# The causal mask of a decayed attention on GpSimd instead of TensorE, and new order weights for both attentions

## The reference

```python
att = softmax(where(causal, q @ k.T / 4, -inf))        # first attention
y   = (att * decay_weight_matrix(T)) @ v               # 1 - (lag/496)**(1/e) behind 15 ones, 0 from lag 511
x   = x + y @ W_proj
x   = x + ffn(layernorm(x))                            # binarized weights, GELU, 1024 hidden
x   = x + layernorm(causal_attention(layernorm(x)) @ Wo + bo) * gamma + beta
x   = x + ffn(layernorm(x))
```

## Time and profile before

| | us |
|---|---|
| median of 3 runs | 2536.53 (2535.64 to 2544.38) |
| the profiled execution | 2545.83 |
| its span, first to last instruction | 2544.1 |
| PE, DVE, ACT, POOL busy | 2319.2, 1961.9, 1469.6, 1020.4 |
| first attention, 150 to 1092 | 942 |
| second attention, 1405 to 2294 | 889 |

### The profile page before, as it was taken

One profiled execution on the slowest core, in us unless ns is written; L12 is line 12 of the kernel. 1 busy time (PEld: TensorE's weight loads), 2 busy tenths in 40 slices (PEclk: granted clock), 3 DMA queues, 4 the chain that ended last, 5 costly groups with the idle time before them and its releaser, 6 DMA issues. The chain is left out here.

```text
span 2544.1 us, 49747 instructions
## 1 busy us (share of the span) xinstructions
PE 2319.2 (91%) x16288; PEld 1345.7 (53%) x16288; DVE 1961.9 (77%) x4826; ACT 1469.6 (58%) x3293; POOL 1020.4 (40%) x1269
## 2 busy tenths in 40 slices
PE   4979999999999989969997799999999998994887
PEld 2545555555555545547765455455454554443666
DVE  5668888888888869756663799898898895914886
ACT  1228687785867777523332357777777776671333
POOL 0038789887878867922211101010010010014452
PEclk8979999999999989989998789999999999996999
DMA  4662122130302140043324611230221314003210
GB/s 153 245 174 68 36 61 64 36 89 11 85 19 77 53 96 11 10 131 119 118 97 134 137 37 42 54 90 23 77 68 32 86 50 104 6 13 120 67 42 33
DMA packets 161902, 188.67 MB, mean 74 GB/s; under 512 B 69360, under 2 KB 92656, under 8 KB 160880
## 3 DMA queue, kind: packets, MB, share of 16 engines
q1 hardware_dynamic: 160304, 180.25, 25.1%
q10 hardware_dynamic: 1344, 5.24, 0.6%
HBM read 114.37 MB, written 69.99 MB: 72 GB/s over the span
## 5 line engine op out<-in xcount | busy, mean ns | idle before, releaser
L886 POOL TENSOR_TENSOR att_a_wd<-att_a_wt,decay 128x256 f32<-128x256 f32 (+3 forms) x896 | 748.4, 872 | 183.4 <-ACT att_a_wt L913 90.9
L913 ACT ACTIVATE att_b_wt<-att_b_ps 128x512 f32<-128x512 f32 (+3 forms) x1280 | 586.7, 542 | 263.9 <-PE att_b_ps L1045 261.5
L953 DVE TENSOR_REDUCE att_a_mpart<-att_a_pm 128x1 f32<-128x512 f32 x768 | 497.5, 683 | 72.7 <-PE att_a_pm L1025 71.4
L953 DVE TENSOR_REDUCE att_b_mpart<-att_b_pm 128x1 f32<-128x512 f32 x768 | 493.8, 683 | 56.9 <-PE att_b_pm L1025 55.5
L913 ACT ACTIVATE att_a_wt<-att_a_ps 128x512 f32<-128x512 f32 (+3 forms) x896 | 415.6, 516 | 182.6 <-PE att_a_ps L1045 178.8
L896 POOL TENSOR_SCALAR_AFFINE_SELECT att_b_wt<-att_b_wt 128x512 f32<-128x512 f32 x128 | 81.3, 635 | 797.5 <-ACT att_b_wt L913 797.5
L1045 PE MATMUL att_b_ps<-att_b_mx,ones_row 64*128 64x512 f32 (+3 forms) x1280 | 364.9, 370 | 0.0
L1025 PE MATMUL att_a_pm<-att_a_kop,att_a_qop 64*128 64x512 f32 (+3 forms) x1024 | 313.5, 423 | 23.7 <-DMA att_a_qop<-qk 12.6
L1038 PE MATMUL att_b_ps<-att_b_qop,att_b_kop 64*128 64x512 f32 (+3 forms) x1024 | 331.9, 434 | 1.4 <-ACT att_b_wt L913 0.7
L1025 PE MATMUL att_b_pm<-att_b_kop,att_b_qop 64*128 64x512 f32 (+3 forms) x1024 | 291.5, 391 | 14.5 <-DMA att_b_qop<-qk 11.4
L1073 PE MATMUL att_b_po<-att_b_wt,att_b_va 128*17 128x512 f32 (+3 forms) x2560 | 292.9, 535 | 0.9 <-POOL att_b_wt L896 0.7
(11 more groups left out here) (183 smaller groups left out, 3540.4 us busy)
## 6 DMA issues: line engine op xcount, KB each, us to landing
att_a_kop<-qk SPq DMA_DIRECT2D x224, 64.0 KB, 2.9
att_b_kop<-qk SPq DMA_DIRECT2D x224, 64.0 KB, 2.9
att_a_qop<-qk SPq DMA_DIRECT2D x216, 64.0 KB, 3.0
att_b_qop<-qk SPq DMA_DIRECT2D x216, 64.0 KB, 2.9
qk<-qkv_a_qk_hi SPq DMA_DIRECT2D x8, 1024.0 KB, 4.0
qk<-qkv_a_qk_lo SPq DMA_DIRECT2D x8, 1024.0 KB, 6.4
y<-att_a_y SPq DMA_DIRECT2D x32, 256.0 KB, 2.3
y_ahead<-y SPq DMA_DIRECT2D x32, 256.0 KB
```

The source lines that it names most:

```text
L886: pool.tensor_tensor(wd[:, v % WD, h, a:z], wt[:, v % buffers, h, a:z], keep["decay"][:, u:u + z - a], ALU.mult).then_inc(w_decayed, 1)
L913: act.activation(wt[:, v % buffers, h, a:CH], pe_[:, n % EBANKS, 0:CH - a], ACT.Exp)\
L953: dve.tensor_reduce(mpart[:, g % 2, c, piece, u:u + 1], pm[:, n % MBANKS, 0:w], AX.X, ALU.max, negate=True).then_inc(m_reduced, 1)
```

## The change

In the decayed attention the mask matmuls go, with the tiles `tri` and `identr`. ScalarE exponentiates the unmasked scores, and GpSimd sets the part above the diagonal of a diagonal block to 0, for four heads at once, as it already does in the other attention. It therefore waits for all four exponentials of such a block, selects, waits for its own select, and then multiplies the four heads by the decay. Blocks off the diagonal are multiplied head by head as before. PO waits for the select on diagonal blocks. The class `Plan` gets the new steps of GpSimd and loses the mask matmuls, and its weights are others.

```diff
-MAXIMUM, FAR, EXP = 75.0, 690.0, (60.0, 0.84)
-TUNED = {True: (100.0, 2, 0.51, (800.0, 200.0, 200.0, 300.0), 0.1, False),
-         False: (30.0, 4, 0.56, (500.0, 200.0, 200.0, 300.0), 0.2, False)}
+MAXIMUM, FAR, EXP = 100.0, 790.0, (170.0, 0.714)
+TUNED = {True: (200.0, 7, 0.49, (400.0, 200.0, 200.0, 0.0), 0.0, False),
+         False: (0.0, 2, 0.51, (300.0, 0.0, 200.0, -600.0), 0.0, True)}
...
         @block.gpsimd
             for item in PLAN:
-                if item[0] == "X" and decayed:
-                    _, g, n, c, kb, h = item
-                    v = n // GH
-                    a, z, u = band_columns(c, kb)
-                    pool.wait_ge(e_weights, n + 1 + EBANKS)
-
-                    pool.wait_ge(pv_done, max(0, v + 1 - WD) + buffers)
-                    pool.tensor_tensor(wd[:, v % WD, h, a:z], wt[:, v % buffers, h, a:z],
-                                       keep["decay"][:, u:u + z - a], ALU.mult).then_inc(w_decayed, 1)
...
+                if item[0] != "X":
+                    continue
+                _, g, n, c, kb, h = item
+                v, diagonal = n // GH, kb >= TB * c
+                if diagonal and n % GH < GH - 1 or not decayed and not diagonal:
+                    continue
+
+                pool.wait_ge(e_weights, n + 1 + EBANKS)
+                if diagonal:
                     pool.sem_inc(w_turn, 1)
-                    block = wt[:, n // GH % buffers, :, P * (kb - TB * c):P * (kb - TB * c + 1)]
+                    block = wt[:, v % buffers, :, P * (kb - TB * c):P * (kb - TB * c + 1)]
                     pool.affine_select(out=block, in_=block, compare_op=ALU.is_ge, fill=0.0, base=0,
                                        pattern=[[0, GH], [1, P]], channel_multiplier=-1).then_inc(w_masked, 1)
+                if decayed:
+                    a, z, u = band_columns(c, kb)
+                    if diagonal:
+                        pool.wait_ge(w_masked, MASKED[v])
+                    pool.wait_ge(pv_done, max(0, v + 1 - WD) + buffers)
+                    for j in range(GH) if diagonal else (h,):
+                        pool.tensor_tensor(wd[:, v % WD, j, a:z], wt[:, v % buffers, j, a:z],
+                                           keep["decay"][:, u:u + z - a], ALU.mult).then_inc(w_decayed, 1)
...
                 if kind == "X":
-                    for i in range(2 if decayed and kb >= TB * c else 0):
-                        tri = keep["tri"][rows, (0, 1, 2, 0)[2 * (h // (GH // 2)) + i], :]
-                        pe.matmul(pe_[:, n % EBANKS, HALF * i:HALF * (i + 1)], tri, keep["identr"][rows, rows],
-                                  start=False, stop=False)
                     mm = pe.matmul(pe_[:, n % EBANKS, 0:CH - a], keep["ones_row"][rows, :], mx[rows, par, c, j, a:CH],
                                    start=False, stop=True)
...
                     pe.wait_ge(e_weights, GH * (v + 1) + EBANKS)
                     if first:
                         pe.wait_ge(o_kept, done(g, c))
+                    if kb >= TB * c:
+                        pe.wait_ge(w_masked, MASKED[v])
```

More of the change, by code:

```diff
@@ L137, in _ @@
             pool.memset(ident[:, :], 0.0).then_inc(zeroed, 1)
-            pool.memset(identr[:, :].bitcast(F32), 0.0).then_inc(zeroed, 1)
-            pool.memset(keep["tri"][:, :, :].bitcast(F32), 0.0).then_inc(zeroed, 1)
             pool.memset(keep["ones_row"][:, :].bitcast(F32), 1.0).then_inc(zeroed, 1)
@@ L142, in _ @@
             pool.memset(keep["ones_strip"][:, HD:STRIP], 1.0).then_inc(zeroed, 1)
-            pool.wait_ge(zeroed, 7)
-            for m in (ident, identr):
+            pool.wait_ge(zeroed, 5)
+            for m in (ident,):
                 pool.affine_select(out=m[:, :], in_=m[:, :].bitcast(F32), compare_op=ALU.not_equal, fill=1.0, base=0,
@@ L149, in _ @@
                                fill=MASK, base=0, pattern=[[-1, P]], channel_multiplier=1).then_inc(ident_ready, 1)
-            for n, base in enumerate((0, HALF, -HALF)):
-                pool.affine_select(out=keep["tri"][:, n, :], in_=keep["tri"][:, n, :].bitcast(F32),
-                                   compare_op=ALU.is_ge, fill=MASK, base=base, pattern=[[-1, P]],
-                                   channel_multiplier=1).then_inc(ident_ready, 1)
         @block.vector
@@ L588, in subtract @@
         a = P * max(0, kb - TB * c)
-        diagonal = self.decayed and kb >= TB * c
-        end = self.run(HEADS[k] // (GH // 2), start, CH - a + 2 * diagonal * (HALF + 48))
+        end = self.run(HEADS[k] // (GH // 2), start, CH - a)
         ready = max(end, self.done.get(v - self.buffers, 0.0))
@@ L596, in subtract @@
         self.weights[v] = self.act + 100.0
-        if self.decayed:
-            a, z, _ = band_columns(c, kb)
-            self.pool = max(self.pool, self.weights[v], self.done.get(v - self.wd, 0.0)) + 160.0 + 2.1 * (z - a)
-            self.decays[v] = self.pool + 120.0
-        elif kb >= TB * c and k == GH - 1:
+        if kb >= TB * c and k == GH - 1:
             self.pool = max(self.pool, self.weights[v]) + 650.0
             self.weights[v] = self.pool + 120.0
+        if self.decayed and (kb < TB * c or k == GH - 1):
+            a, z, _ = band_columns(c, kb)
+            count = GH if kb >= TB * c else 1
+            self.pool = max(self.pool, self.weights[v], self.done.get(v - self.wd, 0.0)) + count * (160.0 + 2.1 * (z - a))
+            self.decays[v] = self.pool + 120.0
     def product(self, start, kind, v, columns):
```

10 lines of the change are left out of this document (2 added, 8 removed).

## The result

| | us |
|---|---|
| before, median of 11 runs | 2539.16 (2527.28 to 2545.18) |
| after, median of 11 runs | 2552.22 (2550.38 to 2570.41) |
| ratio | 1.0075, 95% interval 1.0051 to 1.0099 |
| after, measured once more beside 20 runs of before | 1.0033, interval 1.0012 to 1.0054 |

The change made the kernel slower, by 0.3 to 0.75%. The forecast was 1.0% faster. The time lies in the predicted range, the sign does not.

What follows compares the result with a forecast made beforehand. The prediction took VectorE to set the pace of both attentions. From the profiled 2545.83 us, -10 (first attention) and -16 (second) gave 2519.8; less 9.3 for the median, the forecast was 2510.5 us, range 2470 to 2565.

Steps and rivals of the forecast that it cites:

- What bounds the kernel: Both attentions: they run at VectorE's pace, with some 11 to 12% lost to uneven feeding by TensorE.
- Second attention, -16 us: Second attention: TensorE's new order saves a quarter of VectorE's 62 us of waiting, 16 us; a loss bounded by +10.
- the 40 us: Second attention: a move of more than 40 us either way would show its reading mis-sized.
- First attention, -10 us: First attention: 112 us of new GpSimd work and waits, less 122 us of closed idle time, gives -10 us.
- The select's 81.3 us: First attention: 128 selects on GpSimd at 0.635 us each add 81.3 us.
- Its self-wait: First attention: GpSimd waits 0.24 us for its own result after each of 128 selects, 31 us, bounds 0 to 61.
- I take four fifths: First attention: of 152 us of GpSimd idle time that can close, four fifths close, 122 us.
- TensorE's relief: First attention: dropping 1024 mask matmuls is worth nothing to 56 us at the stage's end; no term of its own.
- Doubling of the loss: First attention: fuller GpSimd doubles what VectorE's two-input operations lose, +24 us in the even stretch, hidden under GpSimd.
- Setup, 0: Setup: six fewer GpSimd instructions for mask and identity change nothing; without cover under 2 us.
- the third rival: First attention: GpSimd multiplying without a break starves VectorE's two-input operations, +50 us there, 2576 us in all; chance 0.22.
- the order brings nothing: Both attentions: the two effects cancel or the second attention's order gains nothing, 2525 to 2547 us; chance 0.20.

Runs made afterwards that it cites:

- 15: b_order_old with VectorE's plain maxima of the second attention reading 256 of 512 columns; second attention 877.8 us.
- 17: b_order_old with two matmuls of zeros ahead of each subtraction of a diagonal block of the second attention; 2588.54 us, second attention 944.6.
- number 7: b_order_old with two matmuls of zeros ahead of each subtraction of a diagonal block of the first attention; 2576.82 us beside 2537.82 of before.
- after_again: The changed kernel unaltered, measured again against before; ratio 1.0033 (1.0012 to 1.0054), second attention 906.8 us.
- b_weigh_back: The changed kernel with the second attention's weigh put back from 0.0 to 0.2; ratio 1.0114 (1.0091 to 1.0136), second attention 931.6 us.
- number 6: The kernel before, mask matmuls kept, with the new weights and prices in the first attention only; ratio 1.0208, first attention 989.8 us.
- number 8: b_order_old with the first attention's select cut to 8 columns of one head; 2528.82 us beside 2537.82 of before, first attention 919.0.
- b_order_old: The changed kernel with the second attention's weights and prices of before; ratio 0.9938 (0.9916 to 0.9959), measured again 0.9947 (0.9920 to 0.9975).
- b_order_new_only: The kernel before with the new weights and prices in the second attention alone; ratio 1.0076 (1.0055 to 1.0098), second attention 903.8 us.

## Why the prediction was wrong

**What bounds the kernel.** The step that failed is the first one: "today both attentions run at VectorE's pace". It was read from the releasers of VectorE's idle time. But that VectorE waits for TensorE says that TensorE is late. The warning that a full row of pipelined matmuls is no proof was taken for an argument against TensorE; it is none for or against. Runs 15 and 17 show otherwise for the second attention: a quarter of VectorE's work can go from its middle without one matmul more getting done, and 1024 matmuls of zeros cost 57 us. For the first attention number 7 shows that TensorE's work counts there too; whether VectorE's does was not tested.

**Second attention, -16 us; measured +21.6.** Sign and size wrong, and the bound of +10 for a loss too. The term "I take a quarter, 16 us" of VectorE's 62 us of waiting rests on that step: it took a new order of TensorE as a gain for VectorE and put what the order does to TensorE's own waits at nothing. The move of 21.6 us lies under the 40 us that the prediction had set as its sign of being wrong; that sign was too wide. If TensorE sets the pace, an order can only gain by keeping TensorE from waiting. Here are its loads' waits in 500 us of the middle, of before:

```profile
PEld att_b_ps L1038 <- ACT att_b_wt L913: 156.9, 301, 0.9
PEld att_b_po L1073 <- ACT att_b_wt L913: 30.1, 87, 0.4
PEld att_b_po L1073 <- issue: 25.8, 84, 0.4
PEld att_b_ps L1038 <- issue: 6.0, 13, 0.9
PEld att_b_pm L1025 <- DVE att_b_mpart L957: 3.9, 6, 0.9
```

and of after:

```profile
PEld att_b_ps L1033 <- ACT att_b_wt L908: 148.9, 324, 0.9
PEld att_b_po L1066 <- issue: 31.1, 95, 0.4
PEld att_b_po L1066 <- ACT att_b_wt L908: 29.4, 87, 0.4
PEld att_b_pm L1020 <- DVE att_b_mpart L948: 10.0, 19, 0.9
PEld att_b_pm L1020 <- DVE att_b_mpart L952: 9.6, 15, 0.9
```

Together they are 222.7 us before and, with two small rows, 233.2 after. That is 10.5 more: 15.7 more for maxima that wait for their bank, 5.2 less for all the rest. Over the whole stage it is 411 against 439 us, with 24 and 63 for the maxima, and after_again has 438. TensorE does 3813 matmuls for 3920, which is 500 x (1 - 3813 / 3920) = 13.6 us less work. So the waits are of the size of the loss, and the new place is the maxima's bank. That is a match, not a proof: with VectorE's maxima halved those waits are still 13.8 us plus 6.8 of "issue", so they are not there because VectorE is slow, and b_weigh_back is the slowest order with a sum of only 227.8. By groups of heads, told by the ends of their value products, the five groups in the middle take 104.6 us each against 102.0 on average, 13 us in all, and the last two 129 + 97 against 112 + 107, another 7. **Open** is which property of the new list makes the maxima late. Two weights (the preference for closing first, the prices) were not undone alone.

**First attention, -10 us; measured -16.6**, and -10 between the median of 14 profiles (926) and the mean of the two with the old code (938.4 and 933.8), of which the spread of 17 us leaves the size open. Term by term:
- The select's 81.3 us: 81.6. Its self-wait: 128 x 0.08 = 10 us, not 31.
- The records of selects and multiplications overlap a little, so that GpSimd's busy time rose by 75 us (755.61 to 831.06). With the self-wait 86 us were added, not 112.
- "I take four fifths" of 152 us closable idle, 122 us: of 183.4 us of idle time 91.2 are left, and 10 of these are the self-wait. So 102 closed, two thirds of 152, and 86 - 102 = -16, as the stage has it. Both terms came out smaller, by 26 and 20 us, and their difference came out near the forecast because they did so together.
- TensorE's relief was "worth between nothing and 56 us" and no term of the sum. Under the new order it is worth about 43 (number 7), and the new weights with the mask matmuls kept lose 51 (number 6). It belonged in the sum. GpSimd's fullness, on which the sum was built, limits little (number 8).

**VectorE and GpSimd in each other's way.** Doubling of the loss was wrong in sign: lines 964, 972 and 997 average 567, 407 and 494 ns in the even stretch of after, where the earlier trace rows had 675, 460 and 1403. VectorE's busy time in the stage was to go "a little up" and fell by 46 us (800.18 to 754.21) at the same 1979 instructions: these three lines took 73.5 us before and 30.5 after, and one operation alone took 32.66 of the 73.5. What this is worth in time no run prices. Nor did the 32.66 us last "the whole time in which GpSimd multiplied without a break": the operation ended at 1087.39, and GpSimd went on to 1089.00.

```profile
L964 DVE TENSOR_TENSOR att_a_ffactor<-att_a_mneg,att_a_mpart 128x16 f32<-128x16 f32 x18 | 9.7, 567 | 0.4
L997 DVE TENSOR_TENSOR att_a_scol<-att_a_scol,att_a_frow 128x32 f32<-128x32 f32 x11 | 5.4, 494 | 0.0
L972 DVE TENSOR_TENSOR att_a_ffactor<-att_a_ffactor,att_a_fsum 128x32 f32<-128x32 f32 (+1 forms) x12 | 4.9, 407 | 0.0
```

**Setup, 0:** the first attention starts 1.1 us later in this pair and at 150.8 to 152.9 us over all runs, so nothing can be told from it. TensorE's total fell by 14.1 us (2319.2 to 2305.1), under the 133 as said.

**The rivals.** The kernel became slower, but not by the third rival: GpSimd starved nobody. The second, "the order brings nothing", was nearest with its 2525 to 2547 us, and it too allowed for no loss by the order. The missing rival was that the new order can make TensorE wait more.

That the time fell inside the range was luck: the range reached so far up for the sake of the third rival, whose mechanism played no part.

## What to carry to other kernels

An engine that keeps waiting for another is not shown to set the pace by being busy: here VectorE was 89% busy and had a quarter of its work to give away. Before you price a change, ask what a little less and a little more work on each engine would do; where the profile can't answer, keep both answers in the range, and both signs.

When a change bundles an edit with a retuned order for several stages, price each stage apart and take each by itself: here the kernel with the first stage's part alone is 0.5 to 0.6% faster than before on two chips, and the whole is slower. Weights of a planner need to be tried on the very work that they are to order: the same ones cost 51 us in the stage whose mask matmuls were still there.

## What the runs showed of the hardware

A two-input operation of VectorE (line 1002 before, 999 in b_order_old) can be held up over many multiplications of GpSimd. Before it took 32.66 us, 37 multiplications long, and in b_order_new_only, which has the same first attention, 32.71. With a select in GpSimd's row it took 8.86 us in b_order_old:

```profile
1047.08 8.86 DVE L999 TENSOR_TENSOR att_a_scol<-att_a_scol,att_a_frow 128x32 f32<-128x32 f32 x1 [14.98 <-DMA att_a_scol<-att_a_y]
1055.97 0.35 DVE L1001 RECIPROCAL att_a_inverse<-att_a_scol 128x32 f32<-128x32 f32 x1
```
```profile
1040.37 14.93 POOL L893 TENSOR_TENSOR att_a_wd<-att_a_wt,decay 128x128 f32<-128x128 f32 x20
1055.21 0.68 POOL L885 TENSOR_SCALAR_AFFINE_SELECT att_a_wt<-att_a_wt 128x512 f32<-128x512 f32 x1
1055.97 4.95 POOL L893 TENSOR_TENSOR att_a_wd<-att_a_wt,decay 128x512 f32<-128x512 f32 x4
```

It ends at 1055.94, in the 0.08 us in which GpSimd waits for its own select. The 20 traces hold 28 such operations of the first attention that took over 2 us. Of these 26 end 0.03 to 0.05 us behind an instruction after which GpSimd paused for 0.08 us or more. The other two are the 32.66 and the 32.71: they end behind the last multiplication of 256 columns, while four of 128 columns still follow without a pause. So the hold can end without a pause too, and what ends it there is open.

The hold does not always come: in after the longest of the 16 on line 997 took 1.35 us, and one that started within the same row of 20 multiplications took 0.43:

```profile
1026.45 14.90 POOL L891 TENSOR_TENSOR att_a_wd<-att_a_wt,decay 128x128 f32<-128x128 f32 x20
1033.15 0.43 DVE L997 TENSOR_TENSOR att_a_scol<-att_a_scol,att_a_frow 128x32 f32<-128x32 f32 x1 [14.97 <-DMA att_a_scol<-att_a_y]
```

The Trainium skill ("SBUF — State Buffer", section "Who interferes with whom") has the loser blocked for the winner's whole instruction; here it was eight multiplications and a select in one case and 37 multiplications in the other, and why it is one instruction in some cases and many in others is open.

The same 1024 matmuls of zeros cost 31 to 48 us in the first attention (43 against the median) and 57 in the second. That is 42 and 56 ns apiece, with 64 columns each and a weight load of its own.
